# A two-batch transformer stack on one core: the first layer's cross products moved among its first chunks, the ending written out by token halves, and a last norm in two steps

## The reference

```python
x = L0(x, ctx)    # scores (x Wq + bq)(ctx Wk + bk)^T / sqrt(E), softmax over the TOKENS, times values; + x; norm, gamma, beta
x = L1(x, ctx)    # cross-attention, softmax over keys, output product, + x
for l in range(6):                                # L2, 16 heads of 64
    tn = ln(x, norm_g, norm_b); x = mha(tn, tn, sa_*, mask) + x      # self-attention
    tn = ln(x, norm_g, norm_b); x = mha(ctx, tn, ca_*, cross) + x    # cross-attention
    tn = ln(x, pre_g, pre_b);   x = x + relu(tn @ w1 + b1) @ w2 + b2 # 512 hidden features
x = L3(x, ctx)    # as L0, with its own weights
```

## Time and profile before

| | |
|---|---|
| median of 3 runs | 1085.88 us (1084.27 to 1086.04) |
| the profiled execution | 1085.62 us, its span 1083.7 us |
| granted PE clock over the span, mean | 0.988 |
| PE busy | 1031.2 us (95%), 5174 matmul records |
| ACT, DVE, POOL busy | 804.0, 719.8, 391.6 us |

### The profile page before, as it was taken

The page is one execution under the profiler, slowest core; times in us unless marked ns, Lnnn a source line. Parts: engine busy times, 40 slices in busy tenths (PEclk is TensorE's granted clock), DMA queues, the critical chain, the costliest instruction groups (busy, mean ns, idle before and its releaser), DMA issues.

```text
span 1083.7 us, 20569 instructions
## 1 busy us (share of the span) xinstructions
PE 1031.2 (95%) x5174; PEld 610.0 (56%) x5174; DVE 719.8 (66%) x4492; ACT 804.0 (74%) x3518; POOL 391.6 (36%) x404
## 2 busy tenths in 40 slices
PE   8899999999999999999999999999999999999984
PEld 6556555665555656555655555656555566555553
DVE  4565788556778566777765678656677755678744
ACT  4496997676998576898666798666798866699831
POOL 4143443233444233443333344223344323344420
PEclk9899999999999999999999999999999999999997
DMA  8401000003200002200002200001300000000000
GB/s 236 130 10 55 13 21 2 2 1 79 66 21 1 1 2 78 67 2 21 1 1 79 67 1 21 1 1 46 96 5 20 2 1 1 21 1 2 1 1 23
DMA packets 31802, 32.39 MB, mean 30 GB/s; under 512 B 3982, under 2 KB 27710, under 8 KB 30910
## 3 DMA queue, kind: packets, MB, share of 16 engines
q1 hardware_dynamic: 29374, 28.80, 9.5%
q10 hardware_dynamic: 2304, 2.20, 0.6%
HBM read 30.47 MB, written 0.52 MB: 29 GB/s over the span
## 4 chain that ended last, share of the span: by engine, by line
PE 85%; DVE 6%; ACT 4%; issue 3%; POOL 1%; DVEq 0%; DMA 0%; SPq 0%
PE S L1046 23%; PE T L1058 11%; PE sum L1088 10%; PE W L856 8%; PE sum L1072 7%; PE W L880 4%; PE W L911 4%; PE W L798 3%; PE W L835 3%; PE W L818 2%; PE W L813 2%; DVE Pb L1501 2%; PE W L875 2%; DVE XN L1350 2%; ACT Pb L1287 2%
## 5 line engine op out<-in xcount | busy, mean ns | idle before, releaser
L1287 ACT ACTIVATE Pb<-Pb,mn 128x128 f32<-128x128 f32 (+1 forms) x1536 | 561.1, 371 | 39.1 <-DVE mn L1501 38.7
L677 POOL TENSOR_TENSOR Pb<-Pb,rsum 128x512 f32<-128x512 f32 (+2 forms) x336 | 324.3, 969 | 610.7 <-DVE rsum L1509 610.6
L1287 ACT ACTIVATION_READ_ACCUMULATOR Pb<-Pb,mn 128x1 f32 x1536 | 295.2, 192 | 0.0
L1501 DVE CUSTOM_DVE_ANT_0 Pb<-S,late_bias 128x128 f32<-128x128 f32 x768 | 175.9, 286 | 125.9 <-PE S L1046 125.6
L1058 PEld LDWEIGHTS T<-ident,Pb 128*128 128x128 f32 (+2 forms) x1296 | 164.0, 146 | 155.4 <-issue 123.9
L1046 PE MATMUL S<-GV,XT 128*128 128x512 f32 x384 | 200.7, 610 | 1.9 <-DVE mn L1501 0.8
L1058 PE MATMUL T<-ident,Pb 128*128 128x128 f32 (+2 forms) x1296 | 197.2, 273 | 1.4 <-POOL Pb L677 1.4
L1519 DVE COPY PT<-T 128x512 f32<-128x512 f32 (+1 forms) x240 | 155.8, 649 | 59.8 <-PE T L1058 59.7
L1501 DVE CUSTOM_DVE_ANT_0 Pb<-S,cross_bias 128x77 f32<-128x77 f32 x768 | 131.8, 232 | 64.9 <-PE S L1046 62.7
L1088 PE MATMUL sum<-PT,Vc 128*128 128x512 f32 (+2 forms) x264 | 135.1, 601 | 0.2 <-DVE PT L1519 0.2
L1046 PE MATMUL S<-Gc,XT 128*128 128x462 f32 (+1 forms) x288 | 125.7, 521 | 3.5 <-DVE mn L1501 2.1
(11 more groups left out here) (175 smaller groups left out, 1061.7 us busy)
## 6 DMA issues: line engine op xcount, KB each, us to landing
sakv<-in_L_xattn_sa_kv SPq DMA_DIRECT2D x6, 1024.0 KB, 5.4
caq<-in_L_xattn_ca_q SPq DMA_DIRECT2D x6, 512.0 KB, 7.9
saq<-in_L_xattn_sa_q SPq DMA_DIRECT2D x6, 512.0 KB, 6.2
cakv<-in_L_xattn_ca_kv SPq DMA_DIRECT2D x12, 256.0 KB, 8.0
saow<-in_L_xattn_sa_ow SPq DMA_DIRECT2D x6, 512.0 KB, 4.0
w<-in_L_xattn_ff_w SPq DMA_DIRECT2D x12, 256.0 KB, 3.1
caow<-in_L_xattn_ca_ow SPq DMA_DIRECT2D x30, 96.0 KB, 3.1
GV<-in_mask_BxSxS_ik ACTq DMA_DIRECT2D x1, 1536.0 KB, 10.1
```

The costliest lines, as they stand in the source:

```text
L677: nc.gpsimd.tensor_tensor(rows, rows, r, ALU.mult).then_inc(sem(f"{unit.name}_weights"), 1)
L1287: last = nc.scalar.activation(Pb[:, s, t * w:(t + 1) * w], Pb[:, s, t * w:(t + 1) * w], ACT.Exp, bias=mn[:, s, t:t + 1], scale=-1.0, accum ...
L1501: last = nc.vector.tensor_tensor_reduce(out=Pb[:, s, cols], in0=S_ps[n % 2][:, cols], in1=row_bias, scale=1.0, scalar=3.4e38, op0=ALU.add, ...
```

## The change

It has three parts and some tidying.

1. **Tables.** `WEIGHTS0_AT` puts the first layer's ck/cv and cG groups among its first chunks. Of the other tables single entries move by one to three ticks; batch 1's norm after self-attention (`AFTER_S1`) is asked for three ticks earlier, and the copy of batch 0's oT after cross-attention comes two ticks later.
2. **Ending.** Batch 0's L3 scores move up among batch 1's last cross chunks (x3, s3, the exp and the scaling of the values), p3 of batch 0 comes right after the last sum, and everything of batch 1 after its last cross chunk is written out by hand on each engine (`ending`), in halves of 256 tokens, with PSUM banks of their own and filler turns (26, 6, 6 and 12). The last norm is two steps: (X - mean) gamma before the root is there, then times rstd plus beta. Batch 0 is stored whole, batch 1 in two halves.
3. **Semaphores.** L0's bq, Wv and bv share one, L1's five loads one, three columns one, three rows one. A wait for one of them now is a wait for all.

```diff
 LAG = {"out": 3}
 FILL = 3
-CV0_AT = (13, 15, 18, 21, 25, 26)
-CV_AT = (4, 5, 7, 22, 26, 28)
-SELF1_AT = (23, 25, 27, 31)
-SELF0_AT = (18, 18, 26, 28)
-WEIGHTS0_AT = (0, 1, 3, 5, 6, 8)
-WEIGHTS_AT = (23, 25, 30, 32, 33, 33, 35, 35, 37, 37, 40, 40, 42, 42, 45, 44)
-AFTER_S0 = (3, 4, 5, 6, 8, 9)
-AFTER_S1 = (2, 3, 4, 7, 8, 9)
-AFTER_X0 = (0, 2, 3, 4, 5, 7)
-AFTER_X1 = (2, 3, 4, 4, 5, 7)
-LAST_AT = (12, 14, 14, 17, 18, 19)
+CV0_AT = (13, 15, 18, 20, 26, 30)
+CV_AT = (4, 6, 7, 22, 26, 29)
+SELF1_AT = (23, 25, 26, 30)
+SELF0_AT = (18, 18, 26, 29)
+WEIGHTS0_AT = (5, 3, 7, 10, 13, 16)
+WEIGHTS_AT = (20, 25, 30, 32, 33, 33, 35, 35, 38, 38, 40, 40, 43, 42, 45, 45)
+AFTER_S0 = (3, 4, 5, 5, 8, 9)
+AFTER_S1 = (2, 3, 4, 4, 5, 6)
+AFTER_X0 = (2, 2, 3, 4, 5, 7)
+AFTER_X1 = (0, 2, 3, 4, 5, 7)
+LAST_AT = (1, 3, 5, 7)
-            self.feed_forward(j, 1, after, *FEED1)
-            if j + 1 == self.layers:
+            if j + 1 < self.layers:
+                self.after_attention(j, 1, 1, after, AFTER_X1)
+                self.feed_forward(j, 1, after, *FEED1)
+            else:
                 self.last_operands((s1 + 30, s1 + 31, s1 + 33))
-                self.last_attention(0, x1 + FEED0[1] + 4, LAST_AT)
-                self.last_attention(1, after + FEED1[1] + 4, LAST_AT)
+                turned, scores, exps, scaled = (x1 + FEED0[1] + 4 + dt for dt in LAST_AT)
+                self.jobs[turned].append(("x3", self.layers, 0))
+                self.jobs[scores].append(("s3", self.layers, 0))
+                self.late[exps].append(("exp3", 0))
+                self.late[scaled].append(("scale3", 0))
...
         def loaded(s, name):
-            return (sem("L3_in"), 8 * 16) if s == "L3" else (sem(f"{s}_{name}_in"), 16)
+            if s == "L3":
+                return sem("L3_in"), 8 * 16
+            if s == "L1":
+                return sem("L1_in"), 5 * 16
+            if name in ("bq", "Wv", "bv"):
+                return sem("L0_values_in"), 3 * 16
+            return sem(f"{s}_{name}_in"), 16
...
+        def cols2(i):
+            return slice(i * T // 2, (i + 1) * T // 2)
+        def tiles2(i):
+            return slice(TB + i * TB // 2, TB + (i + 1) * TB // 2)
+        HIDDEN_BANKS = [[T_ps[0], W_ps[1], W_ps[2], sum_ps], [T_ps[1], S_ps[0], S_ps[1], W_ps[0]]]
+        OUT_BANKS = [W_ps[1], W_ps[2]]
+        LAST_BANKS = [sum_ps, W_ps[0]]
+        VALUE_BANKS = [T_ps[1], S_ps[1]]
...
+            def store(b, ts):
+                sp.dma_start(out[b].rearrange("(t p) e -> p t e", p=P)[:, ts, :], X[:, b * TB + ts.start:b * TB + ts.stop, :])\
+                  .then_inc(sem("out_done"), 16)
...
+                sp.wait_ge(sem("out_ready"), 1)
+                store(0, slice(0, TB))
+                for i in range(2):
+                    sp.wait_ge(sem("out_ready"), 2 + i)
+                    store(1, slice(i * TB // 2, (i + 1) * TB // 2))
+                sp.wait_ge(sem("out_done"), 48)
...
+            root("start", slice(TB, NT), 2)
+            gp.wait_ge(sem("rows_in"), 3 * 16)
             nc.gpsimd.tensor_tensor(bo1[:], bo1[:], bet["L0"][:], ALU.add).then_inc(sem("bo_beta"), 1)
-            gp.wait_ge(sem("L0_gamma_in"), 16)
             gp.wait_ge(sem("bo_beta"), 1)
-            gp.wait_ge(sem("L0_norm"), B)
+            gp.wait_ge(sem("start_norm"), B)
...
             general = gp.value_load(flag[0:1, 0:1], min_val=0, max_val=1)
+            def ending():
+                for i in range(2):
+                    root("tail", tiles2(i), i + 1)
+                for i in range(2):
+                    gp.wait_ge(sem("tail_norm"), i + 1)
+                    rows = X[:, tiles2(i), :]
+                    nc.gpsimd.tensor_tensor(rows, rows, b2[:, L - 1, :].unsqueeze(1).broadcast_to([P, TB // 2, E]), ALU.add)\
+                      .then_inc(sem("tail_b2"), 1)
+                root("tail", slice(0, TB), 3)
+                for i in range(2):
+                    root("tail", tiles2(i), 4 + i)
             with gp.If(general < 1):
                 decoder(FAST, 0)
+                ending()
...
+            def ending():
+                pe.wait_ge(sem("L3_vo"), 1)
+                token_values("L3", 0, W_ps[0]).then_inc(sem("tail_pred"), 1)
+                for i in range(2):
+                    pe.wait_ge(sem("tail_oT"), i + 1)
+                    for t in range(TB // 2):
+                        c = (i * TB // 2 + t) * P
+                        last = nc.tensor.transpose(T_ps[i][:, t * P:(t + 1) * P], oT[:, 1, c:c + P], ident[:])
+                    last.then_inc(sem("tail_turned"), 1)
+                keep(26)
+                for i in range(2):
+                    pe.wait_ge(sem("tail_norm"), i + 1)
+                    for t in range(TB // 2):
+                        last = nc.tensor.transpose(S_ps[i][:, t * P:(t + 1) * P], XN[:, TB + i * TB // 2 + t, :], ident[:])
+                    last.then_inc(sem("tail_turned"), 1)
+                    keep(6)
+                pe.wait_ge(sem("ff_in"), 32 * L)
+                for i in range(2):
+                    pe.wait_ge(sem("tail_xt"), i + 1)
+                    for f in range(NF):
+                        if i == 1 and f == NF - 1:
+                            pe.wait_ge(sem("tail_x"), 1)
+                        nc.tensor.matmul(HIDDEN_BANKS[i][f][:, 0:T // 2], w1[:, f * P:(f + 1) * P], XT[:, T:2 * T][:, cols2(i)],
+                                         start=True, stop=True).then_inc(sem("tail_h"), 1)
+                for i in range(2):
+                    pe.wait_ge(sem("tail_hidden"), NF * (i + 1))
+                    for t in range(TB // 2):
+                        c = (i * TB // 2 + t) * P
+                        for f in range(NF):
+                            last = nc.tensor.matmul(OUT_BANKS[i][:, t * P:(t + 1) * P], hT[:, f, c:c + P], w2[:, f, :],
+                                                    start=(f == 0), stop=(f == NF - 1))
+                    last.then_inc(sem("tail_out"), 1)
+                for i in range(2):
+                    pe.wait_ge(sem("tail_x"), 2 + i)
+                    for t in range(TB // 2):
+                        last = nc.tensor.transpose(LAST_BANKS[i][:, t * P:(t + 1) * P], X[:, TB + i * TB // 2 + t, :], ident[:])
+                    last.then_inc(sem("tail_turned"), 1)
+                for i in range(2):
+                    pe.wait_ge(sem("tail_xt"), 3 + i)
+                    last = nc.tensor.matmul(S_ps[0][0:M, cols2(i)], Go["L3"][:, 1, :], XT[:, T:2 * T][:, cols2(i)],
+                                            start=True, stop=True)
+                last.then_inc(sem("tail_scores"), 1)
+                keep(12)
+                pe.wait_ge(sem("L3_vo"), 2)
+                for i in range(2):
+                    for t in range(TB // 2):
+                        c = (i * TB // 2 + t) * P
+                        last = nc.tensor.matmul(VALUE_BANKS[i][:, t * P:(t + 1) * P], OP[0:M, 1, c:c + P], vo["L3"][0:M, 1, :],
+                                                start=True, stop=True)
+                    last.then_inc(sem("tail_pred"), 1)
             with pe.If(general < 1):
                 decoder(FAST, 0)
...
             general = act.value_load(flag[0:1, 0:1], min_val=0, max_val=1)
+            def ending():
+                act.wait_ge(sem("fast_attended"), len(FAST.groups))
+                for i in range(2):
+                    nc.scalar.activation(oT[:, 1, cols2(i)], sum_ps[:, cols2(i)], ACT.Identity, bias=small[:, L - 1, 1:2])\
+                      .then_inc(sem("tail_oT"), 1)
+                for i in range(2):
+                    act.wait_ge(sem("tail_turned"), 3 + i)
+                    nc.scalar.activation(XT[:, T:2 * T][:, cols2(i)], S_ps[i][:, 0:T // 2], ACT.Identity,
+                                         bias=small[:, L - 1, 3:4], scale=small[:, L - 1, 2:3]).then_inc(sem("tail_xt"), 1)
+                for i in range(2):
+                    for f in range(NF):
+                        act.wait_ge(sem("tail_h"), NF * i + f + 1)
+                        nc.scalar.activation(hT[:, f, cols2(i)], HIDDEN_BANKS[i][f][:, 0:T // 2], ACT.Relu,
+                                             bias=small[:, L - 1, 4 + f:5 + f]).then_inc(sem("tail_hidden"), 1)
+                for i in range(2):
+                    act.wait_ge(sem("tail_turned"), 5 + i)
+                    nc.scalar.activation(XT[:, T:2 * T][:, cols2(i)], LAST_BANKS[i][:, 0:T // 2], ACT.Copy)\
+                      .then_inc(sem("tail_xt"), 1)
+                act.wait_ge(sem("tail_least"), 1)
+                token_exponential("L3", 1)
             with act.If(general < 1):
                 decoder(FAST, 0)
+                ending()
             with act.Else():
...
             general = dve.value_load(flag[0:1, 0:1], min_val=0, max_val=1)
+            def ending():
+                def variances(ts, eps):
+                    dve.drain()
+                    for t in range(ts.start, ts.stop):
```

(61 more changed lines are left out.)

80 lines of the change are left out of this document (37 added, 43 removed).

## The result

The changed kernel takes 1069.26 us (median of 4 runs, 1068.12 to 1069.73), the kernel before, in the same session, 1085.08 us. The ratio is 0.9852, 95% interval 0.9835 to 0.9870: 15.8 us less. The profiled execution took 1069.66 us, its span is 1067.9 us, and the mean granted clock of PE rose from 0.988 to 0.994.

The account below looks back on a forecast made before the run. PE, busy 95% of the span, was taken as the bound: its work, idle time and half-clock time. Start -7.1, layers -4.0 and ending -6.2 gave -17.3 from 1085.62, so 1068.5 us, range 1061 to 1077.

Parts of the forecast that it names:

- Start: First layer's beginning: reordered cross products save 8.5 us, L0's shared semaphore costs 1.4; net -7.1, between -10 and -1.
- rival 1: At the start: PE's clock falls again after idling about 1 and 1.3 us, 4.9 us return, 1073.4; chance 0.15.
- Layers: All layers: moved table entries shorten PE's waits, less a cost for the earlier norm; -4, bounds -12 and +3.
- The four waits that I added up: In the layers: k for XT -3.1, scores for masks -1.3, ck/cv for a bank -1, earlier norm +1.2 us.
- x3 and s3 ahead: Batch 0's x3 and s3 move ahead of the last sum, where PE bounds the chunks; +1.3 us.
- Ending: After the last sum: halves, p3 moved, clock held up and fewer norm passes; -7.5 us, net -6.2 with x3 and s3.
- The clock falls at the start: At the start: short gaps drop PE's clock again, 4.9 us return, 1073.4; chance 0.15.
- Tables give more or nothing: In the layers: all waits go, -12 and 1060.5, chance 0.12; or none, 1072.5, chance 0.09.
- my case: Whole kernel: the main forecast, 1064 to 1072.5 us; chance 0.50.
- Halves cost like wholes: In the ending: halves cost as much as wholes, -2.1 instead of -6.2, 1072.6; chance 0.08.
- DVE behind POOL's root: At batch 1's self-attention norms: DVE stands 2.95 us each, six layers +17.7, layers' -4 lost, 1090.2; chance 0.04.

Follow-up runs that it names:

- e2: Kernel before with only the two first-layer tables (CV0_AT, WEIGHTS0_AT) changed; 1076.99 us against 1085.13.
- e1: Changed kernel with L0's bq, Wv and bv on semaphores of their own again; 1066.68 us.
- e3: Kernel before in its own order, with 24 filler turns ahead of the second ck/cv group at the start; 1081.43 us.
- e4: Changed kernel with the eight tables of the layers put back, its start and ending kept; 1073.24 us.
- e8: Changed kernel with batch 1's last norm in its old form (normalise, then gamma, then beta), by halves; 1067.38 us.
- e5: Changed kernel with one table, AFTER_S1, put back, so batch 1's norm after self-attention comes three ticks later; 1077.10 us.
- e10: e1 with batch 1's XN after self-attention turned one tick later on PE (AFTER_S1's last number 6 to 7); 1074.58 us.
- e11: e1 with both e10's later XN turn and the second group of the next layer's ck/cv products one tick later; 1076.96 us.
- e7: Changed kernel with its ending in wholes of 512 tokens in place of halves; 1069.91 us.
- e12: e1 with filler turns at the start, eight ahead of the first k and nine ahead of the first ck/cv group; 1065.21 us.

## Why the prediction was right

The forecast was 1068.5 us in a range of 1061 to 1077; it came out at 1069.26. By its terms:

- **Start, -8.5 and +1.4 for the merge.** e2 measures the first as -8.1 to -8.4, e1 the second as +1.1. The route was right too. With the merge taken off, in e1, the first scores came at 41.20 (41.1 forecast), the first mask at 42.76 (42.6), the first exp at 45.04 (44.9) and the tenth turn at 74.21 (74), behind the two waits that rival 1 names (0.96 and 1.12). ACT was the limit as argued: 9.44 of 10 us busy at 60 to 70. One price within it was too high: between 41.0 and 51.3 us PE was busy for 8.8 us, not 9.8, and e3 got 3.6 us back for the clock, not 4.9. The sum didn't use it.
- **Layers, -4.** Here the number came out near by luck. With the clock held the tables are worth 5.9 (e4 against e8). The four waits that I added up don't give that: k's wait went as forecast (-3.1) and half the mask waits (-1.6), but XN waits rose by 3.4 where I took 1.2, and the ck/cv waits rose by 1.1 (I had them fall by 1; of the 5.7 us that I put in the layers 0.7 belong to the start). That is -0.2. PE's idle time fell by 3.2 all the same, since small waits that I left out went as well, for weights, GV and XT ahead of scores; and 2.7 us are in PE's busy time, where I had no term.
- **The clock in the layers, no term.** Two falls of 1.7 us in the profiled execution: +3.4. The trace of before has no such fall between 60 and 1040 us, and the ck/cv wait that they follow grew from 1.19 to 1.44 where I had it shrink.
- **x3 and s3 ahead, +1.3.** Before and e4 have the same tables in the layers and different endings; the stretch from the first h of batch 1 to the last sum is 815.0 and 816.1 us: +1.1.
- **Ending, -7.5.** Measured -7.1. XN turned 4.9 after the last sum (5.0 forecast), h started at 7.0 (6.95) and ended at 10.6 (10.4), out ended at 14.2 (14.1), p3 started at 18.5 (18.5), the last norm step ended at 24.6 (24.7). The difference is the store: 3.2 us from there to the end of the span, not 2.7. One price was wrong: POOL's root takes 0.70 to 0.73 us for two columns, not 1.01 as for four. It hides behind DVE's second half.

The measured terms add up: -8.4 + 1.1 - 5.9 + 3.4 + 1.1 - 7.1 = -15.8. Forecast was -17.3. Start and ending were read right, term by term. In the layers two misses, 1.9 more gain from the tables and 3.4 of loss to the clock, met and left 1.5. With the clock held, the same kernel would by my estimate have taken 3.4 us less than 1069.26, near 1066: in the range as well.

The rivals. *The clock falls at the start*: it did not in the changed kernel's profile, but in those of e4, e5, e10 and e11, and it then cost not the 4.9 that I had priced but 1.2 (in e4 from the first XN turn to the first ck/cv group 6.97 us, in the changed kernel 5.79), since only k, v and G ran slow. *Tables give more or nothing*: more than my case, 5.9, and half of what that rival had; the clock hid it. *Halves cost like wholes*: refuted by e7, they are worth 2.9. The Trainium skill (VectorE: DVE Perf Modes, section "The TRN2 errata — SBUF-src ops pay a fixed extra latency per instruction") has a fixed latency for every instruction. The trace agrees as far as there is a fixed share: DVE's add of 256 columns takes 0.42 us and of 512 columns 0.68, ACT's hT copy 0.47 and 0.69. It does not decide here, because the second half's copy runs beside the next engine's first half. *DVE behind POOL's root*: it did not come. PE waited 3.4 us more for XN over all layers, not 17.7, and with the norm put back later in a set of tables made for the earlier one (e5) the kernel lost 7.8.

## What to carry to other kernels

Where PE is 95% busy, the gain left is in its waits, and a wait's price is its length and, behind some of them, a stretch at half the clock (1.7 us each time here); filler turns into an idle bank cost nothing while PE would wait (e3, e12). A table of job positions has to be moved as a set: one entry moved by one tick cost 7.9 us, because what was next in order needed it. A sum that comes out right does not show that its terms were: hold each term against a run of its own. With an executable whose runs spread by 3 us, compare stretches of traces between fixed points before believing a difference of 1 us between medians.
